# Query and key stacks of the attentions spread over partitions by DMA instead of selection matmuls, and the maxima transposed later in the score ring

## The reference

```
q = (x @ wq + bq).reshape(B, N, 16, 16)
k = (ctx @ wk + bk).reshape(B, Nk, 16, 16)     # ctx is x itself in self-attention (Nk = 1024), else the context (77)
v = (ctx @ wv + bv).reshape(B, Nk, 16, 16)
scores = einsum('bqhd,bkhd->bhqk', q, k) / sqrt(16)      # with a mask over the keys in L1ca
out = einsum('bhqk,bkhd->bqhd', softmax(scores), v) @ wo + bo
```

## Time and profile before

| what | us |
|---|---|
| time, median of 3 runs | 4357.05 (4346.62 to 4368.83) |
| the profiled execution's own time | 4370.4 |
| span of that profile, first to last instruction | 4368.6 |
| PE matmul busy | 3874.2 (89%) |
| ACT busy | 2315.6 (53%) |
| DVE busy | 2125.2 (49%) |
| POOL busy | 712.0 (16%) |
| DMA, of 16 engines | mean 21 GB/s, 92.58 MB |

### The profile page before, as it was taken

How to read it: one execution, slowest core, us unless ns; L and a number is a source line. 1 busy time by engine, 2 the same in 40 slices (tenths; PEclk the granted TensorE clock), 3 DMA queues, 4 the chain that set the end, 5 groups by cost and what they waited for, 6 DMA issues and landing times.

```text
span 4368.6 us, 65300 instructions
## 1 busy us (share of the span) xinstructions
PE 3874.2 (89%) x19697; PEld 2181.3 (50%) x19697; DVE 2125.2 (49%) x3461; ACT 2315.6 (53%) x3970; POOL 712.0 (16%) x448
## 2 busy tenths in 40 slices
PE   6999999789888897889988978889889788998888
PEld 4555655334643474336534643356346543563366
DVE  2112111474367454753475437643754467337645
ACT  2122221476467644775476446755765467647754
POOL 1000000100410241004201410024005110140042
PEclk9989989899999998998999989999999899999999
DMA  3000000200000001000000010000000100010000
GB/s 109 18 22 19 10 19 10 67 2 25 30 11 2 11 30 40 2 25 21 20 2 11 30 39 1 16 30 20 1 11 30 39 1 2 26 39 1 1 30 21
DMA packets 90318, 92.58 MB, mean 21 GB/s; under 512 B 28246, under 2 KB 78364, under 8 KB 89884
## 3 DMA queue, kind: packets, MB, share of 16 engines
q1 hardware_dynamic: 61204, 63.43, 4.5%
q10 hardware_dynamic: 28808, 25.17, 1.8%
HBM read 77.80 MB, written 9.44 MB: 20 GB/s over the span
## 4 chain that ended last, share of the span: by engine, by line
issue 64%; PE 18%; POOL 12%; ACT 3%; DVE 2%; DMA 0%; SPq 0%; POOLq 0%; DVEq 0%; ACTq 0%
PE ps L618 17%; POOL hidl L1645 3%; ACT probs L1300 3%; POOL x L1636 2%; DVE mxh L1546 1%; POOL ql L1663 1%; POOL small L1584 1%; POOL hTl L1591 1%; POOL kl L1663 1%; POOL W2h L1654 1%; POOL W1h L1654 1%; PE ps L1038 1%; PE ps L993 0%; POOL W1l L1656 0%; POOL W2l L1656 0%
## 5 line engine op out<-in xcount | busy, mean ns | idle before, releaser
L1300 ACT ACTIVATE probs<-ps 128x512 f32<-128x512 f32 (+1 forms) x2176 | 1192.3, 636 | 438.9 <-PE ps L618 436.2
L1546 DVE TENSOR_REDUCE mxh<-ps 128x2 f32<-128x1024 f32 x1024 | 1202.6, 1220 | 342.6 <-PE ps L618 337.6
L618 PE MATMUL ps<-probs,v 128*32 128x512 f32 (+1 forms) x4864 | 652.8, 609 | 3.8 <-ACT probs L1300 3.8
L618 PE MATMUL ps<-qs,ks 64*128 64x512 f32 x2048 | 589.8, 430 | 68.3 <-ACT probs L1300 68.3
L1584 POOL TENSOR_TENSOR small<-small 128x4 f32<-128x4 f32 x64 | 66.9, 1046 | 2961.4 <-DVE small L1345 2961.4
L618 PE MATMUL ps<-ks,qs 64*128 64x512 f32 x2048 | 466.2, 459 | 54.1 <-DVE mxh L1546 45.8
L618 PEld LDWEIGHTS ps<-ks,qs 64*128 64x128 f32 x2048 | 187.8, 183 | 507.3 <-issue 281.0
L618 PEld LDWEIGHTS ps<-qs,ks 64*128 64x128 f32 x2048 | 268.6, 184 | 329.2 <-ACT probs L1300 287.5
L618 PE MATMUL ps<-hT,slot 128*128 128x512 f32 x448 | 228.9, 653 | 33.3 <-ACT hT L1105 33.3
L1273 ACT ACTIVATE qs<-ps,cols 128x512 fp32r<-128x512 f32 x320 | 214.0, 688 | 70.2 <-PE ps L618 69.6
L1543 DVE TENSOR_REDUCE mx<-ps 128x4 f32<-128x312 f32 x384 | 164.4, 477 | 145.3 <-PE ps L618 143.1
(11 more groups left out here) (210 smaller groups left out, 6038.3 us busy)
## 6 DMA issues: line engine op xcount, KB each, us to landing
qs<-mrow SPq DMA_DIRECT2D x640, 2.0 KB, 1.7
slot<-in_L_w SPq DMA_DIRECT2D x8, 1024.0 KB, 7.2
slot<-in_L_fc_w SPq DMA_DIRECT2D x8, 1024.0 KB, 5.1
adw<-in_L_adaln_w SPq DMA_DIRECT2D x4, 1536.0 KB, 6.6
xin<-in_x ACTq DMA_DIRECT2D x5, 1024.0 KB, 5.5
x_after_block<-x ACTq DMA_DIRECT2D x20, 256.0 KB, 2.2
xin<-x_after_block ACTq DMA_DIRECT2D x5, 1024.0 KB, 5.5
ew<-in_L_e_w SPq DMA_DIRECT2D x6, 768.0 KB, 13.5
```

What stands on the lines that cost most here:

```text
L618: return pe.matmul(out, lhsT, rhs, start=start, stop=stop)
L1300: ins = act.activation(dst, src, ACT.Exp, scale=SCALE)
L1546: dve.tensor_reduce(mxh[:, z, t, j // 2, j % 2, :], ps[:, a:a + 2, :], AX.X, ALU.max, negate=True).then_inc(dve_done, M.add(dve_done, name))
```

## The change

**The stacks.** `K` steps, `sel`, `kz` and its zeroing are gone. In the new stack a head keeps 64 partitions, but its feature d has the four rows 4d to 4d+3 (`BLOCKS = 4`): block 0 is high times high, block 1 high times rest, block 2 rest times high, block 3 holds the mask row, the maximum row (`MAXROW = 63`, the last) and constants. The weights' columns are reordered on the host (`by_head`) so that the four heads of a group lie on the same 32 partitions of the two feature blocks c. `P` now has ACT write the high part and DVE write the rest straight from PSUM, into one tile `split`; POOL and `whole` have no part in it. SP then moves block by block, `split` to `qk`, partitions 32g to 32g+31 to every fourth partition: three DMAs a group, 12 a half, each with 8 KB on each of 32 partitions in self-attention (queries and keys together, 256 KB) and 4 KB in cross-attention (128 KB); the keys of a cross-attention take 12 more, of 19.5 KB. Constant rows are written by DMAs of 1 MB (`set_rows`: two for each self-attention, one for L3ca) and of 78 KB (`set_key_rows`, with two for the mask in L1ca).

**The products.** `A` uses 63 of the 64 rows. In cross-attention it is four matmuls of 78 columns into two banks instead of two of 156 columns into one, and its ring is two deep instead of four. `S` in cross-attention takes 64 rows for each of two heads instead of 128 rows with zeros.

**The order.** In self-attention the first eight `A` of a group take the first half of the keys. `V` 1 to 3 stand between the first `A` steps. The DVE step that joins the halves (`both`) is a step of its own, and `M` comes after two more `A` steps than before and takes its bank from the ring of the scores. The maxima go out in two DMAs a group and half instead of four. In cross-attention keys and values are projected ahead of the first `T`.

```diff
-        first_slot = GH * TPH + 3
-        for i in range(first_slot):
-            more(i + 1)
-            put(tag, *beside[i:i + 1])
-        rest = beside[first_slot:]
-        for i in range(6):
-            put(tag, *rest[2 * i:2 * i + 2])
-            more(taken + 1)
-        put(tag, ("add",))
-        ahead, rate, lag = taken, (GH * TPH + 1) / NT, 2
+        put(tag, ("P", "k", 0, 1), ("P", "q", 0, 1), ("P", "k", 1, 1))
+        more(1)
+        put(tag, ("P", "q", 1, 1))
+        more(3)
+        put(tag, ("V", 1), ("add",))
+        more(5)
+        put(tag, ("V", 2))
+        more(7)
+        put(tag, ("V", 3))
+        more(GH * TPH + 6 + 3)
+        ahead, rate, lag = taken, (GH * TPH + 2) / NT, 2
...
-                maxima += scores[:2] + turn + scores[2:]
-                turn = [("M", g, n)]
+                maxima += scores[:2] + both + scores[2:4] + turned + scores[4:]
+                turn = [("both", g, n), ("M", g, n)]
...
+                def stack(tag, n):
+                    projected = "q" if ATT[tag][0] else "qk"
+                    sp.wait_ge(dve_done, upto(dve_done, *((tag, "P", which, c, n) for which in projected for c in range(KC))))
+                    for g in range(GROUPS):
+                        for b, (q, k) in enumerate(SOURCES):
+                            if ATT[tag][0]:
+                                dst, src = qk[of_block(b), 0, n, g], split[32 * g:32 * g + 32, q, n]
+                            else:
+                                dst, src = qk[of_block(b), :, n, g], split[32 * g:32 * g + 32, q:k + 1:k - q, n]
+                            sp.dma_start(dst.bitcast(F32), src.bitcast(F32)
+                                         ).then_inc(stack_loaded[g][n], M.add(stack_loaded[g][n], (tag, b), LOADED))
...
+                        pe.wait_ge(rows_loaded, upto(rows_loaded, ROWS_LAST[tag]))
+                        pe.wait_ge(stack_loaded[g][n], upto(stack_loaded[g][n], (tag, 2)))
...
+                            pe.wait_ge(stack_loaded[g][i], upto(stack_loaded[g][i], (tag, 2)))
                             for e in range(2):
-                                r = stacked(e, 0, STACK)
-                                ins = mm(ps[:, a + e, :], qs[r, pair, tt], ks[r, pair, i * HALF:(i + 1) * HALF])
+                                r = stacked(e, 0, MAXROW)
+                                ins = mm(ps[:, a + e, :], qk[r, 0, n, g, c, tt], qk[r, 1, i, g, c, :])
...
+                        hi, lo = sides(name)
+                        dve.wait_ge(act_done, upto(act_done, name))
+                        dve.scalar_tensor_tensor(lo, ps[:, M.where(name), 0:kn], col(bias[0], bias[1] + c), hi.bitcast(F32), ALU.add, ALU.subtract
+                                                 ).then_inc(dve_done, M.add(dve_done, name))
```

More of the change, by code:

```diff
@@ L135, in put, with queries, keys @@
         steps.extend((tag,) + w for w in which)
-    def stack(g, n, k_by):
-        return [k for pair in (2 * g, 2 * g + 1) for k in (("K", "act", "q", pair, n), ("K", k_by, "k", pair, n))]
+    def queries(n):
+        return [("P", "q", c, n) for c in range(KC)]
+    def keys(n):
+        return [("P", "k", c, n) for c in range(KC)]
     def head(kind):
@@ L144, in head @@
             return up[:2], up[2:4], up[4:]
[L145 to L149, removed]
+        return queries(0), keys(0) if kind == "self" else [], [("V", 0)] if kind == "self" else []
     def self_attention(tag, follow):
-        put(tag, ("P", "k", 0, 1), ("P", "q", 0, 1), ("V", 1), ("K", "dve", "k", 0, 1), ("K", "dve", "k", 1, 1))
         maxima, turn = [], []
@@ L250, in after_attention @@
             put(tag, ("o", 2), ("o", 3))
+            put(follow, *first[1:], ("R",), ("N", 1), ("T", 1))
         else:
@@ L277, in mlp @@
         put(tag, ("o", 2), ("o", 3))
-        put(follow, ("T", 0), *first)
-        put(follow, ("R",), *later)
-        second_half(follow, rest)
+        if follow == "L3ca":
+            put(follow, *keys(0), ("V", 0))
+        put(follow, ("T", 0), *first, ("R",), *later, *rest, ("N", 1), ("T", 1))
     tag = MODULES[0][0]
@@ L381, in build @@
         r2_end, at[0] = at[0], r2
[L382 to L385 removed]
+        split = place("split", [P, 4, NH, KC, HALF], F32R)
         assert at[0] <= r2_end
@@ L517, in buffer_of, with sides, of_block @@
             return UNITS[tag].index((tag, "PV", g, n, kt)) % 4
-        def whole_of(name):
-            same_half = [k for k in PASS if k[:2] == name[:2] and k[4] == name[4]]
-            i = same_half.index(name)
-            return 2 * name[4] + i % 2, same_half[i - 2] if i >= 2 else None
+        ROWS_LAST = {"L1sa": ("L1sa", 1), "L1ca": ("L1ca", "mask", 1), "L2sa": ("L2sa", 1), "L2ca": ("L2ca", "keys"), "L3ca": ("L3ca", 0)}
+        QLO, QHI, KHI, KLO = range(4)
+        SOURCES = ((QHI, KHI), (QHI, KLO), (QLO, KHI))
+        def sides(name):
+            _, _, which, c, n = name
+            if which == "k" and KIND[name[0]] == "cross":
+                return ksplit[:, 0, c, :], ksplit[:, 1, c, :]
+            hi, lo = (QHI, QLO) if which == "q" else (KHI, KLO)
+            return split[:, hi, n, c, :], split[:, lo, n, c, :]
+        def of_block(b):
+            return slice(b, P, BLOCKS)
         def maxima_of(tag, g, n):
@@ L942, in _ @@
                         b, act_was, dve_was = take(name, act=name, banks=single())
-                        pe.wait_ge(act_done, upto(act_done, *((ln, "hT", t2 // 2, k) for k in range(KC)), *act_was))
+                        needed = ["kvT"] * (tag == "L3ca") if cross else [(ln, "hT", t2 // 2, k) for k in range(KC)]
+                        pe.wait_ge(act_done, upto(act_done, *needed, *act_was))
                         pe.wait_ge(dve_done, upto(dve_done, *dve_was))
@@ L1547, in _ @@
                                               ).then_inc(dve_done, M.add(dve_done, name))
-                    elif kind == "M" and not cross:
+                    elif kind == "both":
                         g, n = step[1:]
```

292 lines of the change are left out of this document (133 added, 159 removed).

## The result

The changed kernel takes 4452.6 us (median of 4 runs, 4450.5 to 4457.8), the kernel before 4351.8 (median of 4): the ratio is 1.0227, 95% interval 1.0194 to 1.0259. It is slower by 2.3%, where 4.7% less was forecast. The profiled execution took 4450.84 us, with a span of 4449.0.

What follows compares the result with a forecast made beforehand. PE was taken as the bound, busy 3874 of 4369 us. Gains of 128 us (self-attentions), 114 (cross-attentions) and 3 (`sel` load), less 40 for the clock, made 205 us, 4.7%: 4155 us, range 4075 to 4290.

Steps and rivals of the forecast that it cites:

- Clock: Both attentions: granted clock falls about once an attention more often, each fall costing about 2 us: 40 us lost.
- the clock stays low: Rival: clock low through the start of maxima and first units, costing 120 us instead of 40: 4275 us; chance 0.12.
- Cross maxima to the first S: Cross-attention maxima up to the first `S`: DVE is the limit, first maximum waits for the last `P`; net gain 0.5 us.
- Cross units: Cross-attention units: `S` waits less for the maxima's DMAs, as half as many go; gain 2 us each.
- Cross head: Before a cross-attention's first `A`: gain 6 us in L2ca, about 10 in L1ca, 5 in L3ca; 7 on average.
- Self head: Before a self-attention's first `A`: `K` steps go, one projection replaces `V` 1 and two `K` steps; gain 5.2 us.
- Start of maxima: Self-attention, first `A` to first `S`: 27.4 us instead of 33, less half a unit; gain 5.1 us.
- Units and V: Self-attention units: 1.7 us from `V` 2 and 3 leaving them, 4 us from `M` no longer waiting.
- Late stacks: Rival: SP's DMAs from 32 partitions come late; at 2 us a DMA the gain is gone, at 3 4640; chance 0.08.
- No pairing: Rival: 63-row `A` matmuls stop overlapping, 0.23 us more each in the units, 193 us in all: 4345 us; chance 0.04.
- PEclk at 0.5 through the starts: Sign that the forecast is wrong: PE's granted clock at 0.5 throughout the starts of the attentions.

Runs made afterwards that it cites:

- e1: Kernel before, with cross-attention score matmuls reading 64 partitions instead of 128: 4443.5 us against 4347.8, ratio 1.0205.
- e5: Changed kernel with cross-attention maxima and scores over 128 partitions (padded keys), two 156-column maxima matmuls, ring four deep: 4361.0 us, ratio 1.0019 to the kernel before.
- e11: Changed kernel, L1sa's fixed-row DMAs issued behind the weight loads and only after context and mask landed: 4414.9 us, ratio 1.0141 to the kernel before.
- e7: Changed kernel, with `both` and `M` no longer taking places in the self-attentions' list of maxima: 4378.7 us, ratio 1.0084 to the kernel before.
- e4: As e3, plus two added matmuls ahead of each self-attention maxima step before the first score: 4863.8 us, ratio 1.1118 to the kernel before.
- e3: Changed kernel plus idle matmuls in cross-attentions, one ahead of each maxima step, two ahead of each score step: 4692.0 us, ratio 1.0768 to the kernel before.
- e2: Changed kernel with padded keys, so cross-attention scores contract over 128 partitions, maxima still over 63: 4431.0 us, ratio 1.0202 to the kernel before.
- e9: Changed kernel, L1sa's two fixed-row DMAs issued last on SP's queue, behind the weight loads: 4460.9 us, ratio 1.0224 to the kernel before.

## Why the prediction was wrong

The sum was 205 us of gain; the medians show 101 us of loss, and the traces 107 behind the mixture of experts. By the prediction's own steps:

- *Clock* (-40 for it). The step that failed. The term took a fall to cost "about 2 us of PE's work", once an attention more often. The fall was seen rightly, its length was not: in a cross-attention, from the first `A` to the last `S`, the clock is low for 43 us on the mean instead of 6. e1 puts the score phases and what follows at 96 us, and e5 the maxima, together with the form of `A`, at 37. I had looked only at `A` when I asked what keeps the clock up, and not at `S`, whose columns stay the same while its partitions are halved. No row of the kernel before had cross scores over 64 partitions; the self-attentions' `S`, over 64 at clock 1.00, would have spoken against a fall.
- The clock is not the whole miss. With 133 us in place of 40 the sum would still have been 112 us of gain. The rest are the terms of the self-attentions and of the heads, below.
- *The rival "the clock stays low"* was nearest in mechanism (chance 0.12), but named the starts of maxima and `A`. Its number was also added up wrongly: 120 in place of 40 gives 4235, not 4275. The starts are DVE's anyway (27.42 of 29.90 us in the row of L1sa).
- *Cross maxima to the first S* (0.5 of gain forecast): 4.0 of loss. e5 takes 3.1 of it back, with the old form of `A` at the same low clock.
- *Cross units* (2 of gain): 5.2 of loss, the clock. The waits on the maxima's DMAs did go, as forecast, and with the clock back the 2 us are there: 20.9 against 22.9 in e5.
- *Cross head* (7 of gain on average): right for L2ca alone, where from the last `S` to the first `A` 33.1 became 27.4; I had written 33 to 27. L1ca gained the same 5.8, of about 10 forecast, L3ca about 1 of 5.
- *Self head* (5.2): missed. In L1sa the 2 MB of fixed rows take it: with them held back (e11) the way from the last `S` of L3ca to the first `A` is 58.8 us, 4.7 less than before. In L2sa the first `A` waits 2.42 us, where I had 4 us of DMA under 8 of PE. The landing is 5.3 us and not 2.2, the pace 1.23 to 1.46 and not under 1.0, and the twelve projection matmuls take 7.11 instead of 5.4 us. There too 2 MB of fixed rows and a weight load are issued just ahead, and no run separates them from the stacks' own pace. Of the fixed rows the prediction says nothing: a step that the diff adds and that I had left unpriced.
- *Start of maxima* (5.1): 2.1 on the mean, 3.2 in L1sa and 1.1 in L2sa, where the second half of the keys costs 1.70 us of waiting. DVE is the limit as said, but its maxima have more gaps than I had put in.
- *Units and V* (5.7): 2.2 of loss. `M` waits no more, as said; the places in the list took it back, and with them mended (e7) the gain is 6.4. At the end of a self-attention the transposes of `aT`, now in the score ring, wait for `probs`, in e7 too:

```profile
1023.56 1.09 PE L1070 MATMUL ps<-ident,tok 128*128 128x128 f32 x8 [1.55 <-ACT probs L1315]
```

- *Late stacks* (rival, from 2 us a DMA): it did not decide, at 1.23 to 1.46 us a DMA PE waits 28.1 us. *No pairing* of 63 rows: it fell, `A` pairs in the units take 456 ns a matmul against 451 before.
- What would show it wrong had "PEclk at 0.5 through the starts": there it was 0.67 to 0.79, and 0.5 where I did not look.

The Trainium skill (TensorE: Matmul & The Clock Gate, Part 1) puts the low level down to an idle stretch, and by that alone the clock would have stayed up. Here the trace disagrees: 0.50 with PE busy for 27.81 of 27.90 us. In e4 a fall came right behind a wait, but it did not end when the wait did.

## What to carry to other kernels

Before taking matmuls off TensorE or narrowing them, look at the granted clock of the stretch they leave behind: it can fall there, and a stretch that is bound by PE then pays for it (here 22.9 us became 28.7, e1). Zeros in unused partitions can be cheaper than leaving them out. Before adding a matmul, take its price from a row of the same kind of matmul, not from its columns (e3). Before reading a difference of two profiles, subtract a stretch that the change leaves alone: here the mixture of experts scattered by 27 us, a quarter of the effect. When a wait is removed in a kernel whose order is a list handed out at a rate, recount the list; and price every DMA that the diff adds, also those that nothing waits for, by what else moves at that time.

## What the runs showed of the hardware

- In L1ca of the second pass, scores over 64 partitions stand at a granted clock of 0.50 to 0.54, over 128 partitions, half of them zeros, at 0.75 to 0.86 with the same columns (before, after, e1, e2, e5). The self-attentions' units, with `A` and `S` over 63 or 64 partitions beside a `PV` over 128, stand at 0.98 to 1.00.
- The same instructions of one kernel took 47.2 us at a granted clock of 0.51 and 27.7 at 1.00, with PE busy for 45.94 and 26.44 us of it (e4).
- A DMA of 256 KB from 32 neighbouring partitions to 32 spread ones takes 1.23 us of its queue's time in L1sa and 1.46 in L2sa, and lands 5.3 us after issue (median).
- 2 MB of transfers inside the chip delayed small loads on another queue: the context's load came 12.1 instead of 5.7 us after the stores. With the 2 MB last on their own queue the delay moved to the loads behind it (e9); with the 2 MB held back until the small loads had landed it was gone (e11).
- One added matmul over 128 partitions and 256 columns, of the kind that `V` uses, takes 0.62 us between pairs over 63 partitions at clock 1.00 (e3); in a row of `V` it is 0.47.
